# Three of ten frames of the edge lists placed with signs from TensorE and ScalarE instead of VectorE's one-hots

## What is computed

```python
def _ngcf_conv(x, W1, W2, src, dst, n_nodes):
    deg_out = clip(segment_sum(ones, src), 1.0)
    deg_in = clip(segment_sum(ones, dst), 1.0)
    norm = rsqrt(deg_out[src] * deg_in[dst])
    h_src, h_dst = x[src], x[dst]
    msg = (h_src @ W1 + h_src * h_dst @ W2) * norm[:, None]
    return x @ W1 + segment_sum(msg, dst)

h = relu(_ngcf_conv(x, W1_1, W2_1, src, dst, n))
h = _ngcf_conv(h, W1_2, W2_2, src, dst, n)
out = layernorm(x + h)
```

## Time and profile before

| | |
|---|---|
| median of 3 runs | 1199.54 us (1197.84 to 1202.66) |
| the profiled execution | 1202.84 us |
| its span, first to last instruction | 1201.2 us |
| mean granted TensorE clock | 0.84 |
| busy share: TensorE 70%, VectorE 84%, ScalarE 62%, GpSimd 67% | |
| first gather of layer 0 | 130.06 us |

### The profile page before, as it was taken

How to read it: one execution, slowest core, us unless ns; L and a number is a source line. 1 busy time by engine, 2 the same in 40 slices (tenths; PEclk the granted TensorE clock), 3 DMA queues, 4 the chain that set the end, 5 groups by cost and what they waited for, 6 DMA issues and landing times. The chain is left out here.

```text
span 1201.2 us, 33258 instructions
## 1 busy us (share of the span) xinstructions
PE 839.4 (70%) x12938; PEld 774.2 (64%) x12938; DVE 1005.9 (84%) x2592; ACT 745.7 (62%) x2759; POOL 801.1 (67%) x819
## 2 busy tenths in 40 slices
PE   1565167878778687778677277767778787777775
PEld 0565156767667676677677276767677677776775
DVE  8999468979998988989877468889779888878767
ACT  2100037778777778777777146676667777766765
POOL 6000577777777777777773577777777777777771
PEclk9999987878887888878777678888878888888886
DMA  6995312222223222222222323444434444444443
GB/s 138 184 257 214 118 27 54 67 67 66 68 54 81 53 67 68 66 68 67 66 67 65 81 50 83 92 94 92 91 75 94 95 91 92 92 94 91 94 94 69
DMA packets 148617, 106.57 MB, mean 89 GB/s; under 512 B 115880, under 2 KB 128616, under 8 KB 147948
## 3 DMA queue, kind: packets, MB, share of 16 engines
q1 hardware_dynamic: 122872, 71.19, 21.6%
q0 software_dynamic: 25472, 32.86, 14.7%
q10 hardware_dynamic: 116, 0.40, 0.1%
HBM read 59.27 MB, written 45.11 MB: 87 GB/s over the span
## 5 line engine op out<-in xcount | busy, mean ns | idle before, releaser
L635 POOL DMA_INDIRECT c_rows<-table,k_row_i x796 | 780.2, 980 | 375.4 <-issue 241.9
L655 PE MATMUL c_sum<-c_rows,c_sel 128*128 128x64 bf16 x4665 | 212.7, 222 | 111.1 <-DMA c_rows<-table,k_row_i 101.4
L672 PE MATMUL c_out<-k_wcat,c_uvt 128*128 128x64 f32 x1568 | 227.4, 307 | 86.7 <-ACT c_uvt L727 85.2
L672 PEld LDWEIGHTS c_out<-k_wcat,c_uvt 128*128 128x128 f32 x1568 | 218.2, 221 | 106.8 <-ACT c_uvt L727 102.7
L655 PEld LDWEIGHTS c_sum<-c_rows,c_sel 128*128 128x128 bf16 x4665 | 208.1, 118 | 116.6 <-issue 111.9
L719 ACT ACTIVATE c_sum<-c_sum,k_xh 128x64 f32<-128x64 f32 x752 | 161.9, 309 | 162.6 <-DVE c_sum L883 162.6
L843 DVE TENSOR_SCALAR c_sel<-k_place,k_grid 128x512 bf16<-128x512 f16 (+2 forms) x796 | 240.9, 372 | 10.2 <-PE c_sum L655 10.2
L712 ACT ACTIVATE c_own<-k_xh 128x64 f32<-128x64 f32 x784 | 201.1, 389 | 9.9 <-PEq L84 7.7
L727 ACT ACTIVATE c_uvt<-c_turn 128x512 f32<-128x512 f32 x196 | 106.4, 595 | 156.1 <-PE c_turn L679 155.8
L655 PE MATMUL c_sum<-c_yr,c_sel 128*128 128x64 bf16 x1555 | 178.8, 209 | 32.6 <-DVE c_lo L856 32.3
L655 PEld LDWEIGHTS c_sum<-c_yr,c_sel 128*128 128x128 bf16 x1555 | 163.5, 111 | 33.8 <-issue 33.6
(11 more groups left out here) (145 smaller groups left out, 996.2 us busy)
## 6 DMA issues: line engine op xcount, KB each, us to landing
table<-c_y SPq DMA_DIRECT2D x48, 384.0 KB, 2.7
c_rows<-table,k_row_i POOLq DMA_INDIRECT x796
c_res<-in_x SPq DMA_DIRECT2D x48, 256.0 KB
out<-c_y SPq DMA_DIRECT2D x48, 256.0 KB, 2.6
table<-k_xh SPq DMA_DIRECT2D x2, 3640.0 KB, 10.6
table<-k_xh SPq DMA_DIRECT2D x1, 3542.5 KB, 11.7
table<-k_xh SPq DMA_DIRECT2D x1, 1040.0 KB, 7.0
table<-k_xh SPq DMA_DIRECT2D x1, 520.0 KB, 5.5
```

The source lines that it names most:

```text
L635: nc.gpsimd.indirect_dma_start(out=rows[:, b % RING, i], out_offset=None, in_=tables[l], in_offset=bass.IndirectOffsetOnAxis(ap=k.row_i[:, ...
L655: last = nc.tensor.matmul(p_sum[g % BANKS][:, t - GROUP[g][0], :], sel[:, b % 2, i, n * P:(n + 1) * P], part[:, i], start=first and q == 0 ...
L672: last = nc.tensor.matmul(p_out[g % 2][:, n, :], uvt[:, g % 2, n, :], k.wcat[:, l, :], start=True, stop=True)
```

## The change

Frames become seven of 12, then 8, 4, 2. Frames 1, 3 and 5 are SIGNED: they have no one-hots. Instead, in 72 units of four raws each, TensorE subtracts by one matmul (`diff`) the lane number 0 to 127 from the target lane of each edge, for four raws at once (512 columns, fp32 in PSUM). Its weights are the lane array before the transposes, with a row of ones below it, and its moving operand is a constant list `pick`. ScalarE takes Sign of this plus 0.5 into a f16 tile (`signs`, ring of 6), and TensorE uses the four 128x128 parts as weights in place of one-hots. The bank then holds sums over lanes: so ScalarE copies it out (`lift`), and TensorE multiplies by a matrix that takes half the difference of neighbouring lanes (`undo_sums`) into bank 4, from which VectorE adds.

TensorE's queue interleaves the units with the placements of the other frames: one unit for every 4.4 raws between raw 48 and raw 360 (`UNIT_AT`), with `diff` five units ahead. Lifts, undos and differs have fixed places. Bank numbers become f % 4, the spread buffers three. GpSimd makes `pick` (4608 columns by 99 rows: a list, a select over all of it, later one select for each signed frame) and `undo`. `lanes` is made later, behind `shifted`. The parts of the table become 93, 96, 96, 80, 16 and 11 tiles. VectorE sets two constants more (a row of ones and 0.5) and has a new order of its steps.

```diff
-FRAME_PS = [14] * 6 + [8, 4, 2]
+FRAME_PS = [12] * 7 + [8, 4, 2]
+SIGNED = (1, 3, 5)
-PIECES = [(k, b, 4) for k in range(7) for b in (0, 4)] + [(7, 0, 8), (8, 0, 8)]
+PIECES = [(k, b, 4) for k in (0, 2, 4, 6, 7) for b in (0, 4)] + [(8, 0, 8), (9, 0, 8)]
+UNITS = [(f, b, q) for f in SIGNED for b in range(EB) for q in range(FRAME_PS[f] // 4)]
+UNIT_RING, AHEAD = 6, 5
+UNIT_AT = [48 + 22 * u // 5 for u in range(len(UNITS))]
+FIRST_DIFFS = {10: 2, 20: 3, 30: 4}
+UNDO_AT = {165: 0, 266: 1, 376: 2}
+LIFT_AT = {27: 0, 51: 1, 72: 2}
+NUMBER_AT = {40: 0, 63: 1}
+ROOT_AT = {47: 0, 71: 1}
-NORM_FRAMES = [1, 3, 5, 6, 7, 8]
+NORM_FRAMES = [1, 3, 5, 7, 8, 9]
+DIFFER_AT = {205: 0, 310: 1, 420: 2}
...
             G.tensor_copy(ident16[:, :], k.ident[:, :]).then_inc(consts, 1)
-            G.iota(lanes[:, :, :], pattern=[[1, P], [0, FRAME_PS[0]]], ...).then_inc(consts, 1)
+            n = FRAME_PS[1]
+            G.iota(pick[:, :, :], pattern=[[0, n * len(SIGNED)], [-1, P]], ...).then_inc(pick_step, 1)
+            pool.wait_ge(pick_step, 1)
+            G.affine_select(out=pick[:, :, :], in_=pick[:, :, :], compare_op=ALU.is_ge, fill=0.0, ...).then_inc(pick_step, 1)
             pool.wait_ge(dst_in, 48)
             G.tensor_scalar(shifted_i, d_i[:, 0:RUN], float(-SHIFT * P), None, ALU.add).then_inc(shifted_made, 1)
+            G.iota(lanes[:, :, :], pattern=[[1, P], [0, FRAME_PS[0]]], ...).then_inc(consts, 1)
...
+            pool.wait_ge(pick_step, 2)
+            for i, f in enumerate(SIGNED):
+                part = pick[:, n * i:n * i + n, :]
+                G.affine_select(out=part, in_=part, compare_op=ALU.not_equal, fill=1.0, ...).then_inc(pick_made, 1)
...
+            def diff(u):
+                f, b, q = UNITS[u]
+                i = SIGNED.index(f)
+                pe.wait_ge(pick_made, i + 1)
+                if u == 0:
+                    pe.wait_ge(carry_made, 1)
+                elif u == 1:
+                    pe.wait_ge(copied, 5)
+                else:
+                    pe.wait_ge(signs_made, u - 1)
+                j = i * FRAME_PS[f] + 4 * q
+                nc.tensor.matmul(bank[DIFF_BANK[u % 2]][:, :], lane_rows[:, b * P:(b + 1) * P], pick[:, j:j + 4, :].rearrange("p j l -> p (j l)"),
+                                 start=True, stop=True).then_inc(diff_made, 1)
...
+            def place_unit(u):
+                f, b, q = UNITS[u]
+                if u % FRAME_UNITS == 0:
+                    clear(f)
+                pe.wait_ge(signs_made, u + 1)
+                for r in range(4):
+                    last = put(f, b, 4 * q + r, signs[u % UNIT_RING][:, r, :], u % FRAME_UNITS == FRAME_UNITS - 1 and r == 3)
+                last.then_inc(unit_placed, 1)
+
+            def undo_sums(i):
+                f = SIGNED[i]
+                pe.wait_ge(lifted, i + 1)
...
+                nc.tensor.matmul(unsummed(f), undo[:, :], summed_up[:, :, 0:columns(f)], start=True, stop=True).then_inc(undone, 1)
...
+                for b in range(b0, b0 + nb):
+                    for p in range(n):
+                        last = put(f, b, p, hot[i % 3][:, :, (b - b0) * n + p], ...)
+                        if b == b0 + nb - 1 and p == n - 1:
+                            last.then_inc(piece_placed, 1)
+                        if raw in FIRST_DIFFS:
+                            diff(FIRST_DIFFS[raw])
+                        for u in range(len(UNITS)):
+                            if UNIT_AT[u] == raw:
+                                place_unit(u)
+                                if u + AHEAD < len(UNITS):
+                                    diff(u + AHEAD)
+                        if raw in UNDO_AT:
+                            undo_sums(UNDO_AT[raw])
+                        if raw in DIFFER_AT:
+                            differ(DIFFER_AT[raw])
+                        raw += 1
...
+            def sign(u):
+                act.wait_ge(diff_made, u + 1)
+                if u >= UNIT_RING:
+                    act.wait_ge(unit_placed, u - UNIT_RING + 1)
+                A(signs[u % UNIT_RING][:, :, :].rearrange("p r l -> p (r l)"), bank[DIFF_BANK[u % 2]][:, :], ACT.Sign, bias=half_lane[:, :]).then_inc(signs_made, 1)
+            for u in range(len(UNITS)):
+                sign(u)
+                if u + 1 in LIFT_AT:
+                    lift(LIFT_AT[u + 1])
+                if u + 1 in NUMBER_AT:
+                    number16(NUMBER_AT[u + 1])
+                if u + 1 in ROOT_AT:
+                    deg_root(ROOT_AT[u + 1])
...
             def add(f):
-                dve.wait_ge(piece_placed, LAST_PIECE[f] + 1)
+                if f in SIGNED:
+                    dve.wait_ge(undone, SIGNED.index(f) + 1)
+                else:
+                    dve.wait_ge(piece_placed, LAST_PIECE[f] + 1)
```

More of the change, by code:

```diff
@@ L108, in prepare @@
         ident16, step16, wrap16 = (sb(n, [P, P], F16) for n in ("ident16", "step16", "wrap16"))
+        lane_rows, pick = sb("lane_rows", [EP + 1, RUN], F16), sb("pick", [EP + 1, FRAME_PS[1] * len(SIGNED), P], F16)
+        lane = lane_rows[0:EP, :]
+        signs = [sb(f"signs{j}", [P, 4, P], F16) for j in range(UNIT_RING)]
+        half_lane, undo, summed_up = sb("half_lane", [P, 1]), sb("undo", [P, P]), sb("summed_up", [P, 4, SPAN])
         lanes = sb("lanes", [P, P, FRAME_PS[0]], F16)
@@ L258, in place @@
[L258 to L270 removed]
+                elif f < 4:
+                    pe.wait_ge(copied, max(f, 1))
+                elif f - 4 in SIGNED:
+                    pe.wait_ge(lifted, SIGNED.index(f - 4) + 1)
+                else:
+                    pe.wait_ge(added, f - 3)
@@ L436, in _ @@
             hots(1)
-            for f in range(1, 6):
-                spreads(f)
-                hots(2 * f)
-                add(f - 1)
-                hots(2 * f + 1)
-                if f - 1 in NORM_FRAMES:
-                    degrees(NORM_FRAMES.index(f - 1))
-                if f - 2 in NORM_FRAMES:
-                    norms(NORM_FRAMES.index(f - 2))
-            spreads(6)
-            hots(12)
+            spreads(1)
+            hots(2)
+            spreads(2)
+            hots(3)
+            add(0)
+            spreads(3)
+            hots(4)
+            add(1)
+            spreads(4)
+            hots(5)
+            degrees(0)
+            add(2)
+            spreads(5)
+            norms(0)
+            hots(6)
+            add(3)
+            spreads(6)
+            hots(7)
+            degrees(1)
+            add(4)
+            spreads(7)
+            norms(1)
+            hots(8)
             add(5)
-            hots(13)
-            spreads(7)
+            spreads(8)
+            hots(9)
             degrees(2)
-            hots(14)
+            add(6)
+            spreads(9)
+            hots(10)
             norms(2)
-            add(6)
-            spreads(8)
-            hots(15)
+            hots(11)
+            add(7)
+            row_numbers(0, CHUNKS - 40)
             degrees(3)
-            row_numbers(0, CHUNKS - 40)
             norms(3)
-            add(7)
             add(8)
+            add(9)
             degrees(4)
```

120 lines of the change are left out of this document (81 added, 39 removed).

## The result

| | before | after |
|---|---|---|
| median of the runs | 1199.58 us (4 runs) | 1215.40 us (4 runs, 1212.76 to 1217.26) |
| ratio | | 1.0130 (95% interval 1.0112 to 1.0148) |
| profiled execution, its span | 1202.84, 1201.2 us | 1217.26, 1215.7 us |
| first one-hot of VectorE | 29.93 us | 37.32 us |
| VectorE's last norms end | 123.3 us | 136.85 us |

The kernel became 1.3% slower: 1215.4 us against a forecast of 1194.5 and a range up to 1204.5. The time came in where the forecast looked, ahead of the first gather: that moved by +17.0 us instead of -5.0. The layers moved by -2.4 between the two profiled executions.

The account below looks back on a forecast made before the run. VectorE was taken to bound the lead-in before the first gather, whose shift passes to the end one for one. The walk's -7.0 and the head's +2.0 gave -5.0 us: 1194.5 against 1199.54, eight in ten between 1187.5 and 1204.5.

Parts of the forecast that it names:

- VectorE's own work: Lead-in: fewer, shorter one-hots, one more spreads and add; -18.4 us, an unhindered VectorE ending near 105 us.
- The difference, 230 ns: TensorE in the lead-in: each 512-column diff matmul takes 230 ns with its change of weights, bounds 213 and 260.
- The sign placement, 35 ns: TensorE in the lead-in: 288 placements with contiguous sign tiles as weights take 35 ns each, against 60 for strided one-hots.
- rival 1: TensorE placements: signs load no faster than one-hots, 60 ns instead of 35; end 5.9 us later, 1200.4; chance 0.13.
- The walk: Lead-in queues laid side by side: last unit ends 90.8, VectorE 114.2; lead-in's end moves 128.8 to 121.7, -7.0 us.
- ScalarE: hidden: ScalarE's signs in the lead-in, some 0.5 us each pipelined, stay hidden by TensorE while under 0.635; bounds 0.5 and 0.69.
- Rival 4: ScalarE sets the lead-in's pace, by Sign/Sqrt table loads or 0.69 us a sign; 3.7 to 3.9 later, 1198.3; chance 0.11.
- The head, +2.0: Before the first one-hot: GpSimd's new selects and VectorE in each other's way cost 2.0 us, bounds -2.1 and 9.5.
- Rival 3: Head: GpSimd's selects hold VectorE the full 9.5 us, first one-hot later than 34; +2.5 us, 1202.0; chance 0.11.
- The tail: Lead-in's end: 203 tiles stored behind norms 2 take 17.5 us; SyncE's wait for stores 7 to 8 us.
- wrong in kind: Layers, from the first gather on: the prediction fails in kind if their 1071 us span changes by over 2 us.
- Rival 2: Lead-in: TensorE's clock falls to 1.2 GHz for half the 48 us stretch; 12.8 us later, 1207.3; chance 0.09.

Follow-up runs that it names:

- experiment 4: Changed kernel, with TensorE kept busy by matmuls of zeros (256 columns, results unread) ahead of the units; ratio to the kernel before 1.0093.
- experiment 7: Kernel before the change, with matmuls of zeros (256 columns) ahead of TensorE's own work in the lead-in; ratio 1.0000.
- 1: Kernel before the change, plus only GpSimd's making of the list pick with its selects, which nothing reads; ratio 1.0045, first one-hot at 37.54 us.
- 2: Changed kernel, with pick made by ScalarE copies and one DMA in place of GpSimd selects; ratio to the kernel before 1.0076, first one-hot 32.18 us.

## Why the prediction was wrong

**VectorE's own work: right.** -18.4 was said; 99.5 us from the first one-hot to the end less 24.3 of waits are 75.2, against 93.4 less 0.3: -17.9.

**The difference, 230 ns with bounds 213 and 260: the step that failed.** It measured 400, so a unit took 0.86 us and VectorE waited for the signed sums. "L655 takes 27 ns for 64 columns, so 213 ns" took its pace from 154 us and carried it into a stretch in which TensorE ran at the other level. That the level was the same was read from the granted clock of 1.00. Other rows of before contradict it:

```profile
144.08 0.24 PE L655 MATMUL c_sum<-c_lo,c_sel 128*128 128x64 bf16 x1
144.14 0.24 PE L655 MATMUL c_sum<-c_yr,c_sel 128*128 128x64 bf16 x1
144.19 0.24 PE L655 MATMUL c_sum<-c_rest,c_sel 128*128 128x64 bf16 x1
```

Here, right behind the lead-in, 64 columns take 53 ns, which is 1.2 GHz, in a stretch that also says 1.00; by that pace 512 columns are 427 (an estimate). The same matmuls show both levels 11 us later: they follow each other every 29 ns up to 155.0 us, and every 53 from there on, where the column falls as well (0.66 in the mean of 155 to 160 us, 0.50 from 156 to 157):

```profile
154.97 0.20 PE L655 MATMUL c_sum<-c_rest,c_sel 128*128 128x64 bf16 x1
155.04 0.24 PE L655 MATMUL c_sum<-c_yr,c_sel 128*128 128x64 bf16 x1
155.00:160.00 5.00, 3.58 (x70) 3.42 (x66) 1.16 (x4) 0.00 (x0) 3.78 (x5) 0.66 0.18 30
```

So the rows of the kernel before held the answer. The Trainium skill (TensorE: Matmul & The Clock Gate, section "What's actually happening") gives 1.2 GHz as the default level; experiments 4 and 7 agree. Term: 0.17 by 72 = 12.2 us.

**The sign placement, 35 ns: probably the same step.** It measured 47, between forecast and rival 1's 60: 0.05 a unit, 3.6 us. The 43 ns that the forecast read as the price of the stride were right: a load of signs lasts 123 ns in the mean, one of one-hots 166. What was off is the 96 ns of L655, again taken at 154 us; at 144 us the same load lasts 130. No run places signs at the higher level, so this stays an argument from rows. Contiguous weights do load faster (47 against 64 ns from start to start), so rival 1 is out. The Trainium skill (TensorE: Matmul & The Clock Gate, section "Weight-path perf modes") says that the fast load reads packed or strided weights; it does not follow that both take the same time, and in this trace they don't.

**The walk** was sound with the wrong pace in it. The units could start at 42.5 us plus the 7.4 of the later head (the walk itself was laid without a later head); with 72 of 0.86 and 2.6 of clears, undos and differs that makes 114.4, and the last unit ended at 114.4 to 114.5. VectorE's waits became 24.3 instead of 9.7, in the places named: undone 10.8, root 7.6, differ 5.3.

**ScalarE: hidden, as said.** A sign lasts 0.687 us, but they overlap: where two follow directly, they take 1.25 us together (L439, 90.27), so 0.56 from one to the next, between the bounds of 0.5 and 0.69. Rival 4's price did not arise: one table load of 1.28 us stood between signs (88.79), and Sign and Sqrt needed no other.

**The head, +2.0: mis-sized.** It was +7.4, by 1 and 2. The bounds (-2.1 to 9.5) held it; the choice failed. "VectorE's other operations in this stretch lost little beside GpSimd" holds for GpSimd's lists (IOTA), not for an operation of it that reads as well; L355 beside L212 was the nearest row, and L491 beside its select fared as it did. L504 to L506 lost 3.7 us beside 6.4 us of selects. Rival 3 would have been the better value: 7.4 of its 9.5 us. It came by way of the sign given for it, a first one-hot later than 34 us. The Trainium skill (SBUF — State Buffer, section "SBUF: two separate sides") has that as a lock for the whole instruction; L491's 5.19 us beside a select of 4.62 agree.

**The tail: right.** Behind norms 2 (127.43) the stores ended 18.4 us later, 17.5 said; the wait of 8.2 was said as 7 to 8. Behind VectorE's end that is 8.9 instead of 7.5 us.

**Together** 5.4 of head, 0.5 of VectorE, 14.6 of waits, 1.4 of tail are 21.9 of the 22.0 us between -5.0 and +17.0. The layers gave 2.4 back, over the bound of 2 that I had set for "wrong in kind". Their code is the same. Of the 2.4 us 1.4 go with the executions that were profiled: that of before lay 3.3 us over its median, that of after 1.9. The runs of before alone lie 4.8 us apart (1197.84 to 1202.66), so a change of the layers is not shown, and the bound of 2 on one pair of executions was too narrow to show one.

**The rivals.** What came is 2 and 3 at once. Rival 2 had the right level and the wrong form: it asked for a fall in the middle of the stretch, with the column as its witness, priced it at half the stretch, and gave it 0.09; in fact there was nothing to fall from. It was tested against a column that couldn't show it. And as the rivals were priced one by one, the range ended at 1204.5, where the two together give 1202.0 + 12.8 = 1214.8. That this is so near to 1215.4 is partly luck: rival 2 was priced for half of the stretch and for all terms, while the level held for the whole of it and only differences and signs were slower; the unit grew by 35%, against the 30% taken.

## What to carry to other kernels

Price a new instruction of an engine by the nearest instruction in time on that engine, not by its fastest sight elsewhere; and check the granted clock against start-to-start times of back-to-back matmuls in the same stretch before it carries a term. GpSimd selects that were put beside VectorE's steps cost VectorE 7.0 us of their 11.0, so price them in full until a row with the same pair of operations shows otherwise. And when work is taken off the bound, count what its replacement asks of the other engines: of the runs here the signs paid (-0.36%) only where they needed no pick and no differences and VectorE's order waited for them less.

## What the runs showed of the hardware

- The granted clock can read 1.00 while TensorE is at 1.2 GHz: in these traces it reads 1.00 at either level up to the first fall that it records (the first zeros of experiment 4, 188 ns apart in the mean against 108 later; L655 at 144 us before, 53 ns against 29 at 154). Clears of 256 columns tell the level: 0.38 us at 1.2 GHz, 0.27 at 2.4.
- Placements of 28 columns take 61 to 64 ns from start to start with stepped weights (56 in 3.61 us at either level, experiment 7) and 47 with contiguous ones, seen at 1.2 GHz alone.
- 128-column signs with a bias of their own follow each other every 0.29 to 0.30 us from a plain f32 row (22 in 6.55 us), every 0.429 from every twelfth f16 value. The Trainium skill (ScalarE: Activation LUTs, section "What ACT_TABLE_LOAD costs") gives 280 ns + 0.833 ns a column less 93 of overlap, by which I estimate 0.294; the plain row agrees.
- Single-input integer steps of VectorE (1024 elements) take 1.9 to 2.0 us beside GpSimd's selects instead of 0.7.
